# Score units in the third batch, four accumulations on ScalarE and GpSimd, two combining tiles in attention's first period

## The chip, the cores and the metric

The kernel runs on one core of a Trainium2 chip. The metric is the device time of one execution in microseconds (us), lower is better. The engines have names of their own: TensorE (PE in the profile, with PEld for its weight loads) multiplies matrices, VectorE (DVE) and ScalarE (ACT) work on tiles and can read PSUM, where TensorE writes, GpSimd (POOL) works on tiles in SBUF alone, SyncE (SP) issues most of the DMAs.

## The reference

One macaron block on x of shape (4, 512, 128), in float32:

```python
x = x + 0.5 * ffn(layernorm(x), ...)
x = x + attention(layernorm(x), Wq, Wk, Wv, Wo)
x = x + 0.5 * ffn(layernorm(x), ...)      # the same weights
```

`ffn` is a mixture of eight experts (128 to 128 to 128, SiLU) of which each token takes the two with the largest router probabilities, plus a shared expert with a gate and an up projection whose output is scaled by a sigmoid of its own. All experts are computed for all tokens; the weight of an expert that a token doesn't take is zero. `attention` has 16 heads of 8 columns, is causal, and takes a slope times the distance off each score.

## The kernel before, in words

The work is in three blocks: first feed-forward block, attention, second feed-forward block. Each engine has its own program, written out in order by hand; semaphores connect them. Nothing is reordered by a planner: what stands behind a waiting instruction on its engine waits too.

**A feed-forward block** runs over four batches of 512 tokens (j = 0 to 3 in the first block, 4 to 7 in the second). A batch has nine combining tiles n = 0 to 8 (eight experts and the shared one), numbered i = 9 j + n. For each n TensorE makes a hidden tile two steps ahead (`hidden`, lines 802 to 816, three matmuls of 512 columns), ScalarE applies SiLU (`silu`, L416), TensorE multiplies by the second weight (`combine`, L834, eight matmuls, into one of three banks, `Y_BANK[i % 3]`), and VectorE scales each token's row by its coefficient and adds it onto X (`accumulate`, L632, four operations of 128x128). The semaphore `y_used` counts tiles added; a combining tile waits until the tile three before it was added and its bank is free. `gate_up` (L617) makes the gated input of tile 8. GpSimd computes the coefficients (`route`, `coef`).

**The projections** of attention's first two batches, and a part of the layer norms, are done in between. `PROJECT_PE`, `PROJECT_ACT` and `PROJECT_DVE` say in which step (j, n) each engine does its part. For the second batch of attention: TensorE projects at (3, 3) and (3, 5); ScalarE takes the high part of the result (`high_qk`, L449) at (3, 4) and (3, 6); VectorE subtracts it (`rest_qk`, L675) at (3, 3) and (3, 5); ScalarE takes the middle part (`middle_qk`, L453) at (3, 5) and (3, 7); GpSimd the low part (`low_qk`, L348); SP writes the three parts to DRAM (`write_parts`, L217 to L223) and later reads them back in the layout that the score matmuls want (`read_rows`, L235).

**Attention** runs over 16 groups G of four heads (four groups a batch), in 17 periods n. A period has ten slots i. In each slot `score_pair(n, i)` interleaves, on TensorE, one transposed unit of group n (`scores_t_steps`, L932, whose exponentials ScalarE takes, L477) with one score unit of group n + 2 (`score_steps`, L905, of which VectorE takes the masked row maxima, `maxima`, L700). A score unit is 512 columns in one or two matmuls, and u = 10 G + i. The maxima of a group are split in three bf16 parts by GpSimd (`split_smax`), transposed by TensorE (`transpose_smax`, L918; for group 0 at step (3, 7), for group n + 1 in slot (n, 3)), copied by ScalarE (`copy_smax`, L483; for group 0 at (3, 8)) and written by SP into rows of the queries (`maximum_rows`, L244). The transposed units of a group wait for these rows (`nm_rows`). GpSimd masks the exponentials (L367), TensorE weighs the values with them (`weigh_values`, L964) in the next period, into `O_BANK`, which is bank 5.

**What sets the order around the change.** The score units of groups 0 and 1 (u = 0 to 19) are issued early, inside the fourth batch of the first block: after each step n `early_scores(n)` says how many, by

```python
EARLY_STEPS = {0: 2, 1: 2, 2: 2, 3: 2, 4: 2, 5: 2, 6: 2, 7: 2, 8: 4}
```

They alternate between banks 2 and 7, so a unit waits until the masks of the unit two before it are done. On VectorE the order of a step is: gating (at n = 7), accumulation, other work of the step, statistics of a layer norm (at n = 6), masks of the early units. Attention's period 0 begins on TensorE when all 36 tiles of the first block are added (`pe.wait_ge(y_used, C * B)`, L1004), and its first transposed unit waits for the maximum rows of group 0. On SP the order is: write the parts of batches 0 and 1 (the rows of batch 0 are read in between), `maximum_rows(0)`, and then period by period. Slot (0, 2) also holds the value projection of the first batch (`values`, 12 matmuls), slot (0, 9) the transposes of a layer norm's result.

## Time and profile before

| what | value |
|---|---|
| device time, median of 3 runs | 321.56 us (320.27 to 321.93) |
| the profiled execution: its own time | 318.92 us |
| the profiled execution: span of its instructions | 317.2 us |
| TensorE busy | 285.7 us, 90% |
| VectorE busy | 251.5 us, 79% |
| ScalarE busy | 171.6 us, 54% |
| GpSimd busy | 125.5 us, 40% |
| granted TensorE clock, mean | 0.973 of full |

Busy time is the time in which an engine executes at least one instruction. Matmuls are pipelined and their ends are modelled, so a busy TensorE is not TensorE at its peak. The profile of one execution is read by the page, by the instructions of an engine in order of time, by groups of instructions and by windows; every time of an instruction is counted from the start of the span. The chain of work that ended last runs for 59% of the span on TensorE and for 18% on VectorE. The first block lasts to about 100 us, attention to about 247 us, the second block to the end.

### The profile page before, as it was taken

What the parts mean: (1) busy time and instruction counts of PE and PEld (TensorE: products, weight loads), DVE (VectorE), ACT (ScalarE), POOL (GpSimd) and SP (SyncE); (2) the same over time, 40 slices, a digit from 0 to 9 for tenths busy, and PEclk for the clock granted to TensorE, in tenths of its full rate; (3) what the DMA queues carried; (4) which work ended last, traced back from release to release, by engine and by line L of the source; (5) the groups of instructions that cost most, each with busy time, mean ns of one, the idle gap of its engine ahead of it and who ended that gap; (6) DMA issues with size and microseconds to landing.
All of it is one profiled execution on the core that took longest, in us unless ns stands there. A gap on an engine that the chain in (4) does not pass through costs nothing.

```text
span 317.2 us, 7138 instructions
## 1 busy us (share of the span) xinstructions
PE 285.7 (90%) x2328; PEld 185.2 (58%) x2328; DVE 251.5 (79%) x1049; ACT 171.6 (54%) x326; POOL 125.5 (40%) x255
## 2 busy tenths in 40 slices
PE   0898998989986998999799999999999999999994
PEld 0687886977652534334343344333444798889894
DVE  3659798788999678998788989999522697988775
ACT  2423432532442667977688888787888243334330
POOL 1385255406143225546414544565622352520200
PEclk9999999999997569999999999999999999999999
DMA  6910000650050014421104411110000001000011
GB/s 170 238 27 3 0 2 2 208 166 25 4 198 2 2 54 151 151 54 52 53 19 136 152 54 52 53 55 2 2 4 2 1 2 33 2 21 16 1 33 35
DMA packets 20669, 17.73 MB, mean 56 GB/s; under 512 B 2461, under 2 KB 19421, under 8 KB 20573
## 3 DMA queue, kind: packets, MB, share of 16 engines
q1 hardware_dynamic: 19912, 17.05, 18.0%
q8 instruction: 19, 0.31, 0.4%
q10 hardware_dynamic: 720, 0.23, 0.3%
q14 instruction: 18, 0.14, 0.1%
HBM read 9.74 MB, written 7.34 MB: 54 GB/s over the span
## 4 chain that ended last, share of the span: by engine, by line
PE 59%; DVE 18%; POOL 8%; issue 7%; ACT 4%; DMA 2%; SPq 1%; DVEq 0%; POOLq 0%; ACTq 0%
PE bank L834 14%; PE bank L964 10%; PE bank L932 9%; PE bank L772 7%; DVE X L632 6%; PE bank L774 5%; PE bank L773 5%; DVE masked_s L700 4%; POOL probs L367 3%; DVE stats L569 2%; PE bank L905 2%; DMA X<-in_x 2%; PE bank L974 2%; ACT probs L477 2%; PE bank L987 1%
## 5 line engine op out<-in xcount | busy, mean ns | idle before, releaser
L700 DVE CUSTOM_DVE_ANT_0 masked_s<-bank,causal_sb 128x512 f32<-128x512 f32 (+3 forms) x256 | 109.7, 485 | 12.9 <-PE bank L905 12.8
L477 ACT ACTIVATE probs<-bank 128x512 f32<-128x512 f32 x160 | 89.7, 602 | 27.7 <-PE bank L932 26.8
L632 DVE SCALAR_TENSOR_TENSOR X<-bank,coef,X 128x128 f32<-128x128 f32 x288 | 80.7, 342 | 20.9 <-PE bank L834 14.5
L834 PEld LDWEIGHTS bank<-w_sb,act 128*128 128x128 f32 x512 | 67.7, 193 | 5.6
L834 PE MATMUL bank<-w_sb,act 128*128 128x128 f32 x512 | 68.0, 276 | 0.0
L367 POOL TENSOR_SCALAR_AFFINE_SELECT probs<-probs 128x512 f32<-128x512 f32 x64 | 39.7, 635 | 67.9 <-ACT probs L477 67.9
L905 PE MATMUL bank<-KA,QA 54*128 54x512 bf16 (+3 forms) x256 | 59.2, 318 | 6.7 <-DVE smax L700 6.0
L416 ACT ACTIVATE act<-bank 128x512 f32<-128x512 f32 x72 | 41.8, 594 | 40.1 <-PE bank L774 40.1
L932 PE MATMUL bank<-QA,KA 57*128 57x128 bf16 (+3 forms) x256 | 58.9, 315 | 0.2
L964 PE MATMUL bank<-probs,VA 128*32 128x256 f32 (+2 forms) x640 | 52.6, 396 | 1.4 <-issue 0.9
L772 PE MATMUL bank<-XH,w_hi 128*128 128x512 f32 x88 | 42.8, 486 | 5.1 <-DVE gated L617 2.3
L932 PEld LDWEIGHTS bank<-QA,KA 57*128 57x128 bf16 x256 | 17.2, 96 | 40.3 <-ACT probs L477 21.3
L774 PE MATMUL bank<-XH,w_lo 128*128 128x512 f32 x88 | 35.5, 403 | 0.0
L773 PE MATMUL bank<-XL,w_hi 128*128 128x512 f32 x88 | 35.2, 400 | 0.0
L905 PEld LDWEIGHTS bank<-KA,QA 54*128 54x128 bf16 x256 | 16.5, 96 | 20.0 <-DVE smax L700 18.2
L772 PEld LDWEIGHTS bank<-XH,w_hi 128*128 128x128 f32 x88 | 17.1, 195 | 12.1 <-DVE gated L617 4.8
L964 PEld LDWEIGHTS bank<-probs,VA 128*32 128x32 f32 x640 | 13.9, 109 | 16.9 <-issue 13.7
L700 DVE DVE_READ_ACCUMULATOR2_ANT smax<- 128x1 f32 x256 | 21.1, 83 | 0.0
L774 PEld LDWEIGHTS bank<-XH,w_lo 128*128 128x128 f32 x88 | 16.9, 193 | 4.0
L304 POOL TENSOR_TENSOR above<-above 128x128 f32<-128x128 f32 (+2 forms) x24 | 8.1, 336 | 24.9 <-DVE above L607 23.6
L773 PEld LDWEIGHTS bank<-XL,w_hi 128*128 128x128 f32 x88 | 17.2, 196 | 0.2
L409 ACT ACTIVATE XH<-bank 128x512 fp32r<-128x512 f32 x12 | 7.2, 597 | 18.7 <-PE bank L788 18.7
(77 smaller groups left out, 320.1 us busy)
## 6 DMA issues: line engine op xcount, KB each, us to landing
qk_scratch<-qk_parts SPq DMA_DIRECT2D x8, 384.0 KB, 2.6
QA<-qk_scratch SPq DMA_DIRECT2D x32, 96.0 KB, 2.3
KA<-qk_scratch SPq DMA_DIRECT2D x32, 96.0 KB, 2.3
qk_scratch<-qk_parts SPq DMA_DIRECT2D x8, 256.0 KB, 2.9
qk_scratch<-qk_parts SPq DMA_DIRECT2D x8, 128.0 KB, 2.8
QA<-smaxT SPq DMA_DIRECT2D x64, 3.0 KB
out_x<-X SPq DMA_DIRECT2D x4, 256.0 KB, 2.3
X<-in_x SPq DMA_DIRECT2D x3, 256.0 KB, 6.2
```

The costliest lines, as they stand in the source:

```text
L367: nc.gpsimd.affine_select(out=blk, in_=blk, compare_op=ALU.is_ge, fill=0.0, base=0, pattern=[[0, GH], [1, P]], channel_multiplier=-1).then ...
L416: nc.scalar.activation(act[:, i % 3, :], H_BANK[(HID * j + n) % 2][:, :], ACT.Silu).then_inc(act_ready, 1)
L477: nc.scalar.activation(dst, src, ACT.Exp).then_inc(exp_done, 1)
L632: m = nc.vector.scalar_tensor_tensor(X[:, b * NT + t, :], Y_BANK[i % 3][:, t * P:(t + 1) * P], coef[:, j % 2, t, n:n + 1], X[:, b * NT + t ...
L700: r = nc.vector.tensor_tensor_reduce(masked_s[:, u % 4, off:off + n], bank[:, off:off + n], causal_sb[:, S - n:S], 1.0, -3e38, ALU.add, AL ...
L772: nc.tensor.matmul(dst, w_h, m_h, start=True, stop=False)
L773: nc.tensor.matmul(dst, w_h, m_l, start=False, stop=False)
L774: return nc.tensor.matmul(dst, w_l, m_h, start=False, stop=True)
L834: m = nc.tensor.matmul(Y_BANK[i % 3][:, r], a, w2_sb[:, n, :], start=True, stop=True)
L905: m = nc.tensor.matmul(dst[:, off:off + n], QA[b % 2][r, h // 2, qt * P:(qt + 1) * P], KA[b % 2][r, h // 2, 0:n], start=True, stop=True, s ...
L932: m = nc.tensor.matmul(T_BANK[u % 3][:, off:off + WID[kt]], KA[b % 2][r, h // 2, kt * P:(kt + 1) * P], QA[b % 2][r, h // 2, kt * P:S], sta ...
L964: m = nc.tensor.matmul(O_BANK[32 * hh:32 * hh + 32, q0:q1], VA[b % 2][:, kt, GH * g + hh, :], probs[G % 2][:, hh, at + q0:at + q1], start= ...
```

## The change

It has three parts, and waits that go with them.

1. The early score units are laid out over steps (j, n) instead of steps of the fourth batch alone: one unit after step 7 and two after step 8 of the third batch, and 2, 2, 1, 2, 2, 2, 2, 2, 2 after the nine steps of the fourth. There are 20 as before.
2. The tiles n = 1, 3, 5 and 6 of the fourth batch (`SIDE`) are not accumulated by VectorE. ScalarE scales each into a tile of SBUF (`scale_side`, four activations of 128x128 with a scale per token), one step later, behind the SiLU of that step. GpSimd adds the four to each other (`add_side`, 128x512, three times) and in period 0 adds their sum onto X (`finish_ffn3`, once more 128x512). `y_count(i)` is the number of tiles before i that VectorE adds; all waits on `y_used` go by it.
3. The tiles n = 7 and 8 of the fourth batch (`DEFERRED`) are multiplied by TensorE in period 0, after slots (0, 1) and (0, 4), into bank 5, and VectorE accumulates them one slot later, behind its masks. Period 0 no longer waits for them. The first weighing of values waits until they are added, since it writes bank 5 too; the statistics of the fourth batch's layer norm wait for `finish_ffn3`.

The diff, cut to its core:

```diff
+        gated, side = sb("gated", [P, S]), sb("side", [P, 3, NT, D])
...
-        EARLY_STEPS = {0: 2, 1: 2, 2: 2, 3: 2, 4: 2, 5: 2, 6: 2, 7: 2, 8: 4}
+        EARLY_STEPS = {(2, 7): 1, (2, 8): 2, (3, 0): 2, (3, 1): 2, (3, 2): 1, (3, 3): 2, (3, 4): 2, (3, 5): 2,
+                       (3, 6): 2, (3, 7): 2, (3, 8): 2}
+        SIDE = tuple(C * (B - 1) + n for n in (1, 3, 5, 6))
+        DEFERRED = {(0, 1): C * B - 2, (0, 4): C * B - 1}
+        def y_bank(i):
+            return banks[5] if i in DEFERRED.values() else Y_BANK[i % 3]
+        def y_count(i):
+            return i - sum(s < i for s in SIDE)
...   (GpSimd)
+            def add_side(k):
+                pool.wait_ge(side_scaled, k + 1)
+                if k >= 2:
+                    pool.wait_ge(side_added, k - 1)
+                nc.gpsimd.tensor_tensor(side[:, 0], side[:, 0], side[:, 1 + (k - 1) % 2], ALU.add).then_inc(side_added, 1)
+            def finish_ffn3():
+                pool.wait_ge(side_added, len(SIDE) - 1)
+                pool.wait_ge(y_used, y_count(C * B))
+                xt = X[:, (B - 1) * NT:B * NT, :]
+                nc.gpsimd.tensor_tensor(xt, xt, side[:, 0], ALU.add).then_inc(x_ffn3, 1)
...
                     if kind == 0 and b == B - 1:
                         low_qk(1, 0)
+                        add_side(1)
                         split_smax(0)
                         low_qk(1, 1)
+                        add_side(2)
...
                         layer_norm(ln_index(*after), after[1])
                     if kind == 0 and b == B - 1:
+                        add_side(3)
                         split_smax(1)
...
                     split_smax(n + 2)
+                if n == 0:
+                    finish_ffn3()
...   (ScalarE)
                             silu(C * j + n)
+                        if C * j + n - 1 in SIDE:
+                            scale_side(SIDE.index(C * j + n - 1))
...
+            def scale_side(k):
+                i = SIDE[k]
+                j, n = divmod(i, C)
+                ac.wait_ge(y_ready, i + 1)
+                if k == 0:
+                    ac.wait_ge(coef_ready, j + 1)
+                if k >= 3:
+                    ac.wait_ge(side_added, k - 2)
+                dst = side[:, 0 if k == 0 else 1 + (k - 1) % 2]
+                for t in range(NT):
+                    m = nc.scalar.activation(dst[:, t, :], y_bank(i)[:, t * P:(t + 1) * P], ACT.Copy,
+                                             scale=coef[:, j % 2, t, n:n + 1])
+                m.then_inc(side_scaled, 1)
...   (VectorE)
-                        accumulate(C * j + n)
+                        if C * j + n not in SIDE and C * j + n not in DEFERRED.values():
+                            accumulate(C * j + n)
...
                         maxima(n + 2, i)
+                    if (n, i - 1) in DEFERRED:
+                        accumulate(DEFERRED[n, i - 1])
...   (TensorE)
-                if i >= 3:
-                    pe.wait_ge(y_used, i - 2)
+                if i in DEFERRED.values():
+                    pe.wait_ge(y_used, y_count(i))
+                elif i >= 3:
+                    if i - 3 in SIDE:
+                        pe.wait_ge(side_scaled, SIDE.index(i - 3) + 1)
+                    else:
+                        pe.wait_ge(y_used, y_count(i - 2))
...
-                        combine(j, n)
+                        if C * j + n not in DEFERRED.values():
+                            combine(j, n)
...
-                        if j == B - 1:
-                            for G, k in early_scores(n):
-                                score_pair(G - 2, k)
+                        for G, k in early_scores(j, n):
+                            score_pair(G - 2, k)
...
+                    if G == 0:
+                        pe.wait_ge(y_used, y_count(C * B))
...
                     if n == 0 and i == 0:
-                        pe.wait_ge(y_used, C * B)
+                        pe.wait_ge(y_used, y_count(C * B - 2))
+                        pe.wait_ge(side_scaled, len(SIDE))
                     score_pair(n, i)
+                    if (n, i) in DEFERRED:
+                        combine(*divmod(DEFERRED[n, i], C))
```

## Rows read from the trace of the kernel before

**Rows 1.** The page, the span in 40 slices: granted TensorE clock in tenths

```profile
PEclk9999999999997569999999999999999999999999
```

**Rows 2.** Windows: start:end length, busy PE, PEld, DVE, ACT, POOL, clock, DMA, GB/s

```profile
72.70:83.10 10.40, 10.02 (x66) 7.46 (x64) 9.22 (x35) 2.54 (x5) 5.16 (x11) 1.00 0.00 0
83.10:91.60 8.50, 7.84 (x46) 5.51 (x44) 8.36 (x35) 4.15 (x8) 2.89 (x6) 1.00 0.29 95
91.60:100.50 8.90, 5.86 (x36) 3.55 (x36) 8.86 (x43) 2.07 (x3) 3.66 (x5) 0.92 0.24 90
100.50:111.20 10.70, 10.46 (x54) 5.41 (x52) 7.58 (x39) 6.65 (x12) 3.27 (x8) 0.50 0.00 1
111.20:121.80 10.60, 10.60 (x92) 4.47 (x91) 8.33 (x37) 7.54 (x14) 3.54 (x9) 0.77 0.27 77
121.80:130.70 8.90, 7.87 (x87) 3.10 (x86) 7.12 (x30) 7.28 (x15) 3.97 (x10) 1.00 0.37 116
```

**Rows 3.** VectorE in order of time (start, length), and the masks' group of the page

```profile
75.00 1.13 DVE L632 SCALAR_TENSOR_TENSOR X<-bank,coef,X 128x128 f32<-128x128 f32 x4 [0.89 <-POOL coef L313]
...
77.25 1.12 DVE L632 SCALAR_TENSOR_TENSOR X<-bank,coef,X 128x128 f32<-128x128 f32 x4
78.29 0.68 DVE L700 CUSTOM_DVE_ANT_0 masked_s<-bank,causal_sb 128x512 f32<-128x512 f32 x1
...
89.33 0.69 DVE L675 SCALAR_TENSOR_TENSOR qk_rest<-bank,qk_parts 128x512 f32<-128x512 f32 x1
...
101.56 0.69 DVE L700 CUSTOM_DVE_ANT_0 masked_s<-bank,causal_sb 128x512 f32<-128x512 f32 x1
...
L700 DVE CUSTOM_DVE_ANT_0 masked_s<-bank,causal_sb 128x512 f32<-128x512 f32 (+3 forms) x256 | 109.7, 485 | 12.9 <-PE bank L905 12.8
```

**Rows 4.** TensorE in order of time, third batch

```profile
63.64 1.05 PE L834 MATMUL bank<-w_sb,act 128*128 128x128 f32 x8
64.45 0.48 PE L772 MATMUL bank<-XH,w_hi 128*128 128x512 f32 x1
...
71.08 0.50 PE L772 MATMUL bank<-XH,w_hi 128*128 128x512 f32 x1 [0.94 <-DVE gated L617]
```

**Rows 5.** ScalarE's groups by shape: busy us, mean ns of one

```profile
L477 ACT ACTIVATE probs<-bank 128x512 f32<-128x512 f32 x160 | 89.7, 602 | 27.7 <-PE bank L932 26.8
...
L424 ACT ACTIVATE sl<-shifted 128x32 f32<-128x32 f32 x8 | 1.7, 215 | 0.0
...
L405 ACT ACTIVATE w_hi<-w_raw 128x256 fp32r<-128x256 f32 x1 | 0.4, 400 | 0.0
```

**Rows 6.** Middle part, low part, write of the parts, maximum rows, in order of time

```profile
90.05 0.63 ACT L453 ACTIVATE qk_parts<-qk_rest 128x512 bf16<-128x512 f32 x1 [0.27 <-DVE qk_rest L675]
...
90.76 1.15 POOL L348 TENSOR_TENSOR qk_parts<-qk_rest,qk_parts 128x512 bf16<-128x512 f32 x1 [1.43 <-ACT qk_parts L453]
...
91.94 0.34 SPq L221 DMA_DIRECT2D qk_scratch<-qk_parts  x1
...
92.80 0.47 SPq L223 DMA_DIRECT2D qk_scratch<-qk_parts  x1
94.43 2.84 SPq L244 DMA_DIRECT2D QA<-smaxT  x4
```

**Rows 7.** DMA from 94.4 to 99.4 us, GB/s in 40 slices of 0.125 us

```profile
GB/s 303 320 352 238 17 0 0 0 0 0 0 16 8 0 0 0 0 25 0 0 0 0 25 0 0 0 0 0 25 0 0 0 0 0 0 0 0 0 0 0
```

**Rows 8.** Period 0 in order of time: TensorE, SP, a piece of the chain

```profile
100.53 0.63 PE L932 MATMUL bank<-QA,KA 57*128 57x512 bf16 x1
...
102.57 0.47 PE L772 MATMUL bank<-w_hi,XH 128*128 128x128 f32 x1
...
105.32 0.60 PE L932 MATMUL bank<-QA,KA 57*128 57x512 bf16 x1
...
106.17 0.59 PE L918 MATMUL bank<-id_b,smax 128*12 128x128 bf16 x4 [0.24 <-ACT VA L460]
...
107.29 0.42 PE bank L932 x2
...
107.40 2.69 SPq L244 DMA_DIRECT2D QA<-smaxT  x4
```

More of the change, by code:

```diff
@@ L65, in macaron_block @@
         act = sb("act", [P, 3, S])
-        gated = sb("gated", [P, S])
+        gated, side = sb("gated", [P, S]), sb("side", [P, 3, NT, D])
         qk_rest = sb("qk_rest", [P, 2, S])
@@ L104, in macaron_block @@
         y_ready, y_used = sem("y_ready"), sem("y_used")
+        side_scaled, side_added, x_ffn3 = sem("side_scaled"), sem("side_added"), sem("x_ffn3")
         qk_ready, qk_high, qk_sub = sem("qk_ready"), sem("qk_high"), sem("qk_sub")
@@ L139, in macaron_block, with early_scores @@
         EARLY = 2 * NU
-        EARLY_STEPS = {0: 2, 1: 2, 2: 2, 3: 2, 4: 2, 5: 2, 6: 2, 7: 2, 8: 4}
+        EARLY_STEPS = {(2, 7): 1, (2, 8): 2, (3, 0): 2, (3, 1): 2, (3, 2): 1, (3, 3): 2, (3, 4): 2, (3, 5): 2,
[6 more added lines that the diff above has]
+            return i - sum(s < i for s in SIDE)
         def score_bank(u):
             return banks[(2, 7)[u % 2]] if u < EARLY else banks[(2, 7, 0)[(u - EARLY) % 3]]
-        def early_scores(n):
-            first = sum(EARLY_STEPS[k] for k in EARLY_STEPS if k < n)
-            return [divmod(u, NU) for u in range(first, first + EARLY_STEPS.get(n, 0))]
+        def early_scores(j, n):
+            first = sum(EARLY_STEPS[k] for k in EARLY_STEPS if k < (j, n))
+            return [divmod(u, NU) for u in range(first, first + EARLY_STEPS.get((j, n), 0))]
         def score_units(g):
@@ L263, in _ @@
             for b in range(B):
-                sp.wait_ge(y_used, C * (B + b + 1))
+                sp.wait_ge(y_used, y_count(C * (B + b + 1)))
                 sp.dma_start(out[b].rearrange("(t p) d -> p t d", p=P), X[:, b * NT:(b + 1) * NT, :]).then_inc(stored, 16)
@@ L309, in route @@
                 if j >= 2:
-                    pool.wait_ge(y_used, C * (j - 1))
+                    pool.wait_ge(y_used, y_count(C * (j - 1)))
+                if j - 2 == B - 1:
+                    pool.wait_ge(side_scaled, len(SIDE))
                 nc.gpsimd.tensor_scalar(coef[:, j % 2, :, E], th[:, :], 1.0, 0.25, ALU.add, ALU.mult)
@@ L564, in moments @@
                 elif kind == 1:
-                    v.wait_ge(y_used, C * (b + 1))
+                    v.wait_ge(y_used, y_count(C * (b + 1)))
+                    if b == B - 1:
+                        v.wait_ge(x_ffn3, 1)
                 else:
@@ L629, in accumulate @@
                 if i >= 1:
-                    v.wait_ge(y_used, i)
+                    v.wait_ge(y_used, y_count(i))
                 for t in range(NT):
-                    m = nc.vector.scalar_tensor_tensor(X[:, b * NT + t, :], Y_BANK[i % 3][:, t * P:(t + 1) * P],
+                    m = nc.vector.scalar_tensor_tensor(X[:, b * NT + t, :], y_bank(i)[:, t * P:(t + 1) * P],
                                                        coef[:, j % 2, t, n:n + 1], X[:, b * NT + t, :], ALU.mult, ALU.add)
@@ L666, in ffn @@
                             moments(*after)
-                        if j == B - 1:
-                            for G, i in early_scores(n):
-                                maxima(G, i)
+                        for G, i in early_scores(j, n):
+                            maxima(G, i)
             def rest_qk(b, i):
@@ L833, in combine @@
                     a = gated[:, r] if n == E else act[:, i % 3, r]
-                    m = nc.tensor.matmul(Y_BANK[i % 3][:, r], a, w2_sb[:, n, :], start=True, stop=True)
+                    m = nc.tensor.matmul(y_bank(i)[:, r], a, w2_sb[:, n, :], start=True, stop=True)
                 m.then_inc(y_ready, 1)
@@ L860, in ffn @@
                             part(*of)
-                        if j == B - 1:
-                            for G, k in early_scores(n):
-                                score_pair(G - 2, k)
+                        for G, k in early_scores(j, n):
+                            score_pair(G - 2, k)
                         if j == B:
```

## Prediction, written before the changed kernel was run

> **What bounds the kernel now.** I read the slices of the page first. TensorE's clock is full in all of them but three in a row [rows 1], which is where the first block ends and attention begins; so I read that stretch in windows, stage by stage [rows 2]. In the first half of the fourth batch TensorE is the full engine (10.02 us of 10.40). In 91.6 to 100.5 it is VectorE (8.86 of 8.90), TensorE works 5.86 us, and the clock falls at the end of that stretch (mean 0.92). Attention's period 0 then runs wholly at the lower level, 1.2 GHz (clock 0.50), with TensorE busy 10.46 of 10.70; period 1 gets the 2.4 GHz back about half way (0.77); period 2 needs 8.90 us at full clock. So two things cost time here: VectorE's load before attention, and the slow clock that its starving of TensorE leaves behind. From period 2 on nothing in the diff touches the order except one small GpSimd addition long before its use, so a shift at 121.8 us is a shift of the end.
>
> **The change part by part.** Prices: a tile's accumulation holds VectorE 1.04 us (77.25 to the next mask at 78.29), a score unit's masks 0.69 us (109.7 us over 160 units) [rows 3]. On TensorE a combining tile takes 0.81 us at full clock (63.64 to 64.45) [rows 4].
>
> Units 0 to 2 in the third batch. Unit 0 is issued where TensorE waits 0.94 us for the gated tile anyway [rows 4]: free. Units 1 and 2 stand before the next hidden tile; unit 2 needs the bank of unit 0, so TensorE loses about 0.7 us there, and saves a part of it where the pair stood before, one step later. VectorE's masks fill the 0.89 us that it waits for the coefficients (the accumulation at 75.00) [rows 3] and run over by 0.3 us. All together between 0 and +0.7 us at this place; I take +0.3, which the next part absorbs. The rows that unit 0 reads were issued long before; their last issue of group 0 precedes unit 0 by some 3.7 us.
>
> First half of the fourth batch. TensorE is the bound there, so what VectorE sheds buys nothing. I walked through it tile by tile: each unit waits for the masks two units back, each of the two subtractions of the projection (L675) for TensorE's projection and a ScalarE copy; the second of them, at 89.33 before [rows 3], comes at 89.2. Gain 0.1 us.
>
> Second half. From that subtraction VectorE had 12.2 us to the end of the last early mask (101.56, where the next unit begins) [rows 3]. Of these, three accumulations (3.1 us) and two of the ten units (1.3) are gone; subtraction, statistics and gating stay. 7.8 us, done at 97.0. TensorE issues its last early unit when the mask two before it is done, and is free at 95.9; the first matmul of attention stood at 100.53 [rows 8]. If nothing else held it, this would be -4.6 us, the far end.
>
> What holds it next: the maximum rows of group 0. SP issues them behind the three writes of the second batch's key parts, these wait for GpSimd's low part, that for ScalarE's middle part, and this now stands behind the copy of the fourth side tile, which waits for the combining tile (3,6). By my walk that tile ends at 90.2. Side copy 1.0, and 0.1 until it begins: 91.3. Middle part 0.63: 91.9. Low part 1.15: 93.05. Three issues on SP, 1.33: 94.4 [rows 6]. The rows were issued from 94.43 before, and their four transfers show in the DMA bins up to 98.0, 3.6 us after the first issue [rows 7]. So they land at 98.0 again, hidden before by VectorE, now the last thing that period 0 waits for: start at 98.1, -2.4 us. The GpSimd sums of the side tiles (as large as the low part, so some 1.15 us each) stand behind the low part, or in front of the first split of maxima, which is done some 4 us before TensorE transposes it. I take 0; if the second sum slipped in front of the low part it would be +1.15.
>
> The side copies. No activation of 128x128 is in the trace. Below lies the 128x32 (215 ns), above the 128x256 (400 ns) [rows 5]; I take 0.25 us, nearer the smaller, since neighbours overlap: 1.0 us for a tile of four. Ends: 0.86, with four of the smaller, and 2.4 us, at the 602 ns of 512 columns. Two such tiles stand in the rows' chain (before the second high part, and before the middle part), so the ends move the start of period 0 by -0.3 and +2.8 us.
> The Trainium skill, ScalarE: Activation LUTs, section "What ACT_TABLE_LOAD costs", says that an activation costs 186 ns plus 0.833 ns a column and each per-partition pointer operand some 93 ns more. The first agrees with the 215 ns of the 128x32 row; the side copies carry their scale as such a pointer, which no activation here does. By that page a tile would be 1.2 us (an estimate), the start of period 0 98.5 and the whole 0.4 us less gain.
>
> The waits that come with them. A side copy waits for a combining tile that TensorE issues a hidden tile after the one whose SiLU ScalarE would take next; so that SiLU moves back by the tile and the copy, some 1.8 us. Who needs it is TensorE, a combining tile, a pair and a hidden tile later (0.81, 0.4 and about 0.8 us, and the masks' waits between them): 0, and at most 4 x 0.5 us if the copies reach their upper end. TensorE's waits on the side copies before it takes a bank again, and GpSimd's on the copies, find them done a step earlier. The first weighing of values, in period 1, waits for the second deferred accumulation, which VectorE does half a period before: 0. GpSimd's last addition, 1.15 us, falls in the idle time between its masks of periods 0 and 1.
>
> The two deferred tiles. They put 16 matmuls into period 0: 1.6 us at full clock, 3.3 us at the lower one (half pace), and two accumulations on VectorE, which waited for TensorE in this period and hides them. Bounds 0 and 3.3.
>
> The clock. TensorE is nearly idle from 92.6 to 98.1 in the new order (four units and four transposes in 5.5 us), sparser than the stretch before which the clock fell last time, so it falls again, before period 0 begins. The question is how long it stays. Before, it stayed low through all of period 0 and into period 1. There the tile (0,1) now joins the pairs and the value projection, and the tile (0,4) makes the stretch after the transposes of maxima longer by 1.65 us of dense matmuls (106.7 to 110.1 before). I take it to come back inside period 0.
>
> The sum, by period 0's own rows [rows 8]: start 98.1; two pairs at 0.43 (the chain's 0.42 for a pair's two transposed score matmuls; the first ones waited for masks before, no longer), tile 1.65, pair 0.43, value projection 2.75 (102.57 to 105.32), pair, ScalarE's copy and the transposes (105.32 to 106.17 before): transposes at 104.55. Rows of group 1 issued 1.23 us behind (107.40 against 106.17), landed 3.6 us later: 109.4. Period 1 begins at 109.6 with the clock back at about 107, at 110.7 with it back at the end of period 0, instead of 111.2. Period 1 at full clock: 8.9 as period 2, and 0.6 for its value projection, 9.5 instead of 10.6. Together -2.7 and -1.6; middle -2.2 us. The profiled execution took 318.92 us (span 317.2 and 1.7 around it), 2.6 below the median of the runs, 321.56; I put the shift on the median: 319.4 us. Half a per cent, 1.6 us, is about what a measurement tells from no change.
>
> **The rivals.** (a) The clock stays low as long as before, into period 1. For it: the value projection kept TensorE busy without a break from 102.57 to 105.9 and the clock did not rise. Then transposes at 104.55 leave 1.65 + 6 x 0.43 + 1.1 us of the XN transposes and 0.5 of their own: period 1 at 111.2 as before, later parts alike: 0.0, 321.6 us. Against it: more dense work than before.
> (b) The clock doesn't fall: the rows come as soon as TensorE is free. Period 0 then takes 8.6 us from 98.1 (pairs 0.25, tile 0.81, projection 1.4, ScalarE's copy 0.75, rows' chain 4.85), period 1 9.5: 116.2 for 121.8, -5.6 us, 316.0. Against it: the idle stretch above.
> (c) Slower: ScalarE's side copies sit in front of the second high part and the middle part, and cost the upper end, 2.4 us a tile. The rows land 2.4 to 2.8 us later, the start gains nothing, and the two tiles are paid at the low clock: with 2.4, period 1 at 113.6 and +2.4 us, 324.0. It decides from a start of period 0 later than 99.7. For it: ScalarE takes them in order, and three engines and a queue follow. Against it: the row of 128x256.
> (d) The early units don't get their rows in time in the third batch: the four reads of group 0 come in a stretch where the DMA is busy. TensorE would wait there up to 1 us, where it is the bound: 320.4.
>
> **How the numbers follow.** Forecast 0.55 (its own range 318.1 to 320.6), (a) 0.20, (b) 0.08, (c) 0.12, (d) 0.05. Faster by over 0.5%: four fifths of the forecast, all of (b), some of (d): 0.54. Slower: (c) and a little of (a): 0.14. The rest, 0.32: within. The range takes in (b) with part of the 2.6 us between profile and median, and half of (c): 315.2 to 323.0.
>
> **What would show it.** Right: VectorE's last early mask near 97.0; attention's first matmul near 98.1, released by the maximum rows; the clock low at that moment and full again before period 1 begins near 110; period 1 of 9.5 us; masks and the last statistics unmoved in relation to the periods. Wrong: a start of period 0 before 97 (the rows' chain is shorter than I think) or after 99.7; a clock that never falls, or that is low in half of period 1; side copies of over 0.35 us; the projection's second subtraction later than 90; TensorE waiting for rows in the third batch.

## The result, and the profile of the changed kernel

The changed kernel takes 324.3 us (median of 20 runs, 319.69 to 328.5), the kernel before 321.8 us beside it on the same chip (20 runs, 319.6 to 325.31). Executions of one kernel fall into a faster and a slower kind, and every ratio in this document is that of the faster ones alone, while the medians are those of all. The ratio is 1.0068 (95% interval [1.004, 1.0096]): slower by 0.7%, where 319.4 us and a gain had been forecast. The profiled execution took 322.08 us with a span of 320.3 (before 318.92 and 317.2), so the two traces differ by 3.1 us; the medians differ by 2.5 and the runs, by the ratio, by 2.2. The traces show the sign of the difference and about its size.

The page of the changed kernel, granted TensorE clock in 40 slices of the span, against [rows 1]:

```profile
PEclk9998999999995579999999999999999999999999
```

The low stretch lies in the same three slices (13 to 15) and is deeper in the first of them: the clock falls earlier. (The 8 in the fourth slice lies ahead of everything that the diff touches; the kernel without part 3, below, has a full clock there, and its gated tile of the third batch starts at 72.16 us, here at 72.17.) The windows by stage, cut where the stages of [rows 2] end in the new trace (start:end length, busy PE, PEld, DVE, ACT, POOL, clock, DMA share, GB/s):

```profile
72.90:83.40 10.50, 10.50 (x67) 7.82 (x68) 8.97 (x37) 4.01 (x12) 5.24 (x11) 1.00 0.00 0
83.40:92.00 8.60, 7.74 (x47) 5.48 (x46) 5.91 (x21) 5.14 (x14) 3.24 (x6) 1.00 0.29 94
92.00:99.90 7.90, 3.87 (x19) 1.31 (x18) 6.27 (x35) 3.78 (x8) 6.36 (x7) 0.69 0.27 101
99.90:114.30 14.40, 13.14 (x68) 8.57 (x68) 7.98 (x35) 6.66 (x12) 3.26 (x8) 0.58 0.10 28
114.30:124.90 10.60, 10.52 (x92) 4.37 (x91) 8.93 (x41) 7.46 (x15) 5.27 (x10) 0.84 0.14 41
124.90:133.80 8.90, 7.87 (x87) 3.10 (x86) 7.12 (x30) 7.28 (x15) 3.97 (x10) 1.00 0.35 116
```

The first two stages are about as long as before (10.5 and 8.6 us, 10.4 and 8.5 before). VectorE did get lighter: in the second it is busy for 5.91 us where it was 8.36, in the third for 6.27 where it was 8.86. Yet attention begins at 99.90 instead of 100.53, only 0.63 us earlier, with TensorE busy for 3.87 us of 7.90. Period 0 is 14.4 us long instead of 10.7, period 1 is 10.6 as before, and from period 2 on nothing differs. So -0.63 + 3.74 + 0.0 = +3.1 us: all of the span's difference is there at the start of period 2, and what makes it is period 0.

TensorE in order of time in the changed kernel (start, length, in brackets the idle time before it and what ended that), against [rows 8]:

```profile
99.90 0.58 PE L992 MATMUL bank<-QA,KA 57*128 57x512 bf16 x1 [2.39 <-DMA QA<-smaxT]
...
100.96 2.07 PE L894 MATMUL bank<-w_sb,act 128*128 128x128 f32 x8
102.97 0.60 PE L992 MATMUL bank<-QA,KA 57*128 57x512 bf16 x1
...
108.16 2.07 PE L894 MATMUL bank<-w_sb,gated 128*128 128x128 f32 x8
...
113.40 0.28 PE L965 MATMUL bank<-KA,QA 54*128 54x256 bf16 x1 [1.02 <-DVE smax L753]
...
114.31 0.39 PE L992 MATMUL bank<-QA,KA 57*128 57x512 bf16 x1
...
124.92 0.39 PE L992 MATMUL bank<-QA,KA 57*128 57x512 bf16 x1
```

The lines at 99.90, 114.31 and 124.92 begin periods 0, 1 and 2. Three things are to be seen. Before period 0 TensorE waits 2.39 us with nothing to do, for the maximum rows. The two deferred tiles then hold it for 2.0 us each (100.96 to 102.97, 108.16 to 110.17). And at the end of period 0 it waits another 1.02 us for masks.

The clock over those moments (windows of 2 us, columns as above):

```profile
94.00:96.00 2.00, 0.90 (x4) 0.22 (x4) 2.00 (x10) 1.96 (x3) 1.92 (x4) 0.77 0.35 138
96.00:98.00 2.00, 1.21 (x4) 0.25 (x4) 1.99 (x13) 0.11 (x1) 1.92 (x2) 0.50 0.69 258
...
110.00:112.00 2.00, 2.00 (x18) 0.94 (x17) 1.16 (x6) 1.20 (x3) 0.00 (x0) 0.50 0.02 5
112.00:114.00 2.00, 0.98 (x10) 0.44 (x8) 2.00 (x12) 1.15 (x3) 1.22 (x2) 0.97 0.66 185
114.00:116.00 2.00, 1.92 (x14) 0.49 (x14) 2.00 (x12) 1.91 (x5) 1.08 (x3) 0.89 0.04 12
116.00:118.00 2.00, 2.00 (x19) 0.75 (x22) 2.00 (x8) 0.85 (x2) 1.67 (x4) 0.50 0.00 0
```

The granted clock is at its lower level (0.50, 1.2 GHz) when both deferred tiles run, returns near 112, inside period 0, and falls a second time near 116, after the 112-to-114 window in which TensorE was busy for only 0.98 us.

The wait for the maximum rows is in the chain that ended last (start, length, what), against [rows 6, 7]:

```profile
93.30 1.16 POOL qk_parts L381
...
94.48 0.34 SPq L235
...
95.86 0.78 SPq L258
...
98.06 1.71 DMA QA<-smaxT
...
99.90 0.58 PE bank L992
```

That is the chain the prediction named (low part, three writes, rows), in which every step up to the issue of the rows is 1.3 to 1.5 us later than it was walked: rows issued at 95.86 and not at 94.4. ScalarE shows where that begins:

```profile
88.75 1.14 ACT L492 ACTIVATE side<-bank,coef 128x128 f32<-128x128 f32 x4 [2.49 <-PE bank L894]
89.76 0.61 ACT L500 ACTIVATE qk_parts<-bank 128x512 bf16<-128x512 f32 x1
...
91.56 1.14 ACT L492 ACTIVATE side<-bank,coef 128x128 f32<-128x128 f32 x4 [0.70 <-PE bank L894]
92.57 0.65 ACT L504 ACTIVATE qk_parts<-qk_rest 128x512 bf16<-128x512 f32 x1
```

A side copy, itself waiting for a combining tile, stands in front of the second high part, so that VectorE's second subtraction starts at 90.41 (89.33 before, 89.2 forecast). The next one stands in front of the middle part, and ScalarE waits 0.70 us for its combining tile, (3, 6), before it can begin at 91.56 (90.3 forecast). What made that tile late is told below, where the prediction is gone through.

### The profile page after: what moved, and what is told of

Same layout as the page of the kernel before. It is cut to its first block, busy times and chain, and to the rows that moved or that the text cites. A ratio compares the mean times of both kernels' runs of the same rounds, so it can differ in the third digit from the quotient of the medians.

```text
span 320.3 us, 7144 instructions
## 1 busy us (share of the span) xinstructions
PE 288.2 (90%) x2328; PEld 187.3 (58%) x2328; DVE 247.4 (77%) x1033; ACT 175.5 (55%) x342; POOL 130.4 (41%) x259
## 4 chain that ended last, share of the span: by engine, by line
PE 60%; DVE 14%; POOL 9%; issue 7%; ACT 4%; DMA 2%; SPq 2%; DVEq 0%; POOLq 0%; ACTq 0%
PE bank L894 16%; PE bank L1026 10%; PE bank L992 8%; PE bank L827 7%; PE bank L829 5%; PE bank L828 5%; DVE X L685 5%; DVE masked_s L753 3%; POOL probs L400 2%; DVE stats L622 2%; DMA X<-in_x 2%; PE bank L965 2%; PE bank L1036 2%; ACT probs L528 2%; POOL qk_parts L381 1%
## 5 line engine op out<-in xcount | busy, mean ns | idle before, releaser
L685 DVE SCALAR_TENSOR_TENSOR X<-bank,coef,X 128x128 f32<-128x128 f32 x272 | 76.2, 342 | 20.0 <-PE bank L894 14.4
L894 PEld LDWEIGHTS bank<-w_sb,act 128*128 128x128 f32 x512 | 69.2, 197 | 6.5 <-issue 0.8
L894 PE MATMUL bank<-w_sb,act 128*128 128x128 f32 x512 | 69.5, 280 | 0.0
L992 PE MATMUL bank<-QA,KA 57*128 57x128 bf16 (+3 forms) x256 | 57.9, 311 | 2.6 <-DMA QA<-smaxT 2.4
L827 PEld LDWEIGHTS bank<-XH,w_hi 128*128 128x128 f32 x88 | 17.2, 196 | 10.5 <-issue 4.2
```

Source lines behind the costliest of these rows:

```text
L685: m = nc.vector.scalar_tensor_tensor(X[:, b * NT + t, :], y_bank(i)[:, t * P:(t + 1) * P], coef[:, j % 2, t, n:n + 1], X[:, b * NT + t, :] ...
L827: nc.tensor.matmul(dst, w_h, m_h, start=True, stop=False)
L894: m = nc.tensor.matmul(y_bank(i)[:, r], a, w2_sb[:, n, :], start=True, stop=True)
L992: m = nc.tensor.matmul(T_BANK[u % 3][:, off:off + WID[kt]], KA[b % 2][r, h // 2, kt * P:(kt + 1) * P], QA[b % 2][r, h // 2, kt * P:S], sta ...
```

## The experiments

The theory after the result: parts 1 and 2 (units in the third batch, side copies) help a little and are then held by the maximum rows; part 3 (the two deferred tiles) takes work out of a stretch where TensorE waits and puts it into a period in which it is full, at the lower clock. The main rival: the side copies in the rows' chain are what costs.

Each kernel is compared with the kernel before, run beside it on the same chip, whose median was 321.55 to 321.77 there. Two kernels are compared by their ratios to it; 0.1% is 0.3 us.

### The changed kernel without part 3

```
-        DEFERRED = {(0, 1): C * B - 2, (0, 4): C * B - 1}
+        DEFERRED = {}
-                        pe.wait_ge(y_used, y_count(C * B - 2))
+                        pe.wait_ge(y_used, y_count(C * B))
```

> The changed kernel with its third part undone: tiles 7 and 8 of the fourth batch are multiplied and added in their steps, period 0 waits for them; the early units and the side tiles stay. Theory A (TensorE waits for the maximum rows in front of period 0 anyway, so the two tiles were free where they stood and are paid in full in period 0): first transposed matmul at 100.2 to 101 (99.9 in the changed kernel), period 0 shorter by 3.5 to 4.1 us than its 14.4, no 2.07 us groups of the combining line in it; about -3 us against the changed kernel at a like clock, -0.5 to +0.5 against the one before. Rival (the time follows the low clock alone): period 0 stays near 14 us, the time stays within 1 us of the changed kernel's.

Measured: 320.28 us, ratio 0.9962 [0.9924, 1.0001], so 1.1% or some 3.4 us less than the changed kernel. Its TensorE at the beginning of periods 0, 1 and 2, and its windows before period 0 and in it:

```profile
99.91 0.58 PE L992 MATMUL bank<-QA,KA 57*128 57x512 bf16 x1 [1.57 <-DMA QA<-smaxT]
...
110.04 0.60 PE L992 MATMUL bank<-QA,KA 57*128 57x512 bf16 x1
...
119.94 0.39 PE L992 MATMUL bank<-QA,KA 57*128 57x512 bf16 x1
```
```profile
92.00:99.90 7.90, 5.04 (x35) 3.27 (x34) 7.87 (x42) 3.79 (x8) 6.35 (x7) 0.96 0.27 101
99.90:110.00 10.10, 9.85 (x52) 5.58 (x52) 6.83 (x35) 6.50 (x12) 3.78 (x9) 0.50 0.00 1
```

Period 0 starts at the same moment, released by the same rows: the two tiles fit into the wait in front of it, which goes from 2.39 to 1.57 us. It then takes 10.13 us instead of 14.41, though its clock is low from end to end, and period 1 (to 119.94) 9.9 instead of 10.61. So part 3 costs 4.98 us at the start of period 2, and what it takes away in front of period 0 is worth nothing. It even empties TensorE there (3.87 us busy of 7.90, 5.04 without part 3), and the clock falls at 95.1 instead of 99.2. The rival falls: the side copies are all in here. (Of the 4.98 us the ends of the two traces show 2.0, because this one has low stretches late in attention that the other has not; see what stays open.)

### Part 3 alone, on the kernel before

Against the changed kernel, cut to its core (the waits and sums of the side tiles go too):

```
-        EARLY_STEPS = {(2, 7): 1, (2, 8): 2, (3, 0): 2, (3, 1): 2, (3, 2): 1, (3, 3): 2, (3, 4): 2, (3, 5): 2,
-                       (3, 6): 2, (3, 7): 2, (3, 8): 2}
-
-        SIDE = tuple(C * (B - 1) + n for n in (1, 3, 5, 6))
+        EARLY_STEPS = {(3, 0): 2, (3, 1): 2, (3, 2): 2, (3, 3): 2, (3, 4): 2, (3, 5): 2, (3, 6): 2, (3, 7): 2, (3, 8): 4}
+
+        SIDE = ()
```

> The kernel before with the third part alone: tiles 7 and 8 of the fourth batch go into period 0, VectorE adds them there; early units and the other accumulations as before. Theory A: VectorE's stretch in front of attention loses two accumulations (2.1 us), the rows land near 98.0, first transposed matmul at 98.5 instead of 100.53; period 0 then carries two groups of 2.07 us at the lower clock level and waits once for masks behind an accumulation: 13.5 to 14.4 us instead of 10.67; in all +1 to +2 us against the kernel before at a like clock. Rival (the third part costs only beside the side tiles): within 0.5 us of the kernel before or faster.

Measured: 322.58 us, 1.0052 [1.0022, 1.0082]: slower by itself, within the expected loss. Its profiled execution was an unusually long one (327.6 us), so its periods are not compared with the others (period 0 takes 15.63 us in it, at the lower clock throughout, where 13.5 to 14.4 had been expected). Its beginning is read: the rows are issued at 95.42, a write of the parts ahead of them having taken 1.37 us on SP, and period 0 starts at 99.78, behind the last early units, where 98.5 had been expected. The start was missed; the sign and the size of the loss were not.

### Part 1 alone, and part 2 alone

The first has the new table of early units on the kernel before; the second is the changed kernel with the old table and nothing deferred.

> The kernel before with the first part alone: three score units move into the third batch, the rest is laid out as in the changed kernel. VectorE's stretch between the second subtraction and the end of the early masks loses two units (1.3 us), no accumulation. Theory A: last early mask near 100.2 instead of 101.56, first transposed matmul at 99.2 to 99.6 instead of 100.53, -1.0 to -1.3 us at a like clock. Rival (the third batch pays for what it takes): hidden tiles of the fourth batch start 0.5 us later and stay so, first transposed matmul within 0.4 us of 100.53.

> The kernel before with the second part alone: four accumulations go to ScalarE and GpSimd; units and the last two tiles as before. VectorE loses one accumulation between the second subtraction and the end of the early masks, and three ahead of it, where TensorE is the bound. Theory A: VectorE ends 1.0 us earlier, but the rows, behind two side copies of 1.14 us, are issued at 95.9 and land at 99.5: first transposed matmul at 99.9 to 100.2, -0.4 to -1.2 us at a like clock. Rival (VectorE is the bound up to attention, so that all four count): first transposed matmul at 97 or earlier, -3 us or more.

Measured: 320.77 us each, ratios 0.9955 [0.9917, 0.9994] and 0.9968 [0.9932, 1.0005]. The first transposed matmul of each, part 1 alone and then part 2 alone:

```profile
99.94 0.58 PE L931 MATMUL bank<-QA,KA 57*128 57x512 bf16 x1 [0.48 <-DVE X L633]
```
```profile
99.95 0.37 PE L991 MATMUL bank<-QA,KA 57*128 57x512 bf16 x1
```

Part 1 alone starts 0.3 us later than the 99.2 to 99.6 it was given, part 2 alone within its bounds. Alone, together (99.91) or with part 3 as well (99.90), period 0 starts at 99.9. But the last wait is another one each time: VectorE's last accumulation in the one, the early units just ahead of it in the other, the maximum rows where both are in. By the ratios the gains are 0.5%, 0.3% and, together, 0.4%, each with an interval of some 0.4% to either side: whether they add can't be told from the times. In the traces they do, by the start of period 2, at 121.81 before, 121.16 and 120.69 with one part and 119.94 with both, though the start of period 0 is the same.

### The rows ahead of the second key write on SP's queue

```
             for b in range(2):
                 write_parts(b, 0)
+                if b == 1:
+                    maximum_rows(0)
                 write_parts(b, 1)
 ...
-            maximum_rows(0)
```

> The changed kernel with one edit on SP: the maximum rows of group 0 are issued ahead of the write of the second batch's key parts instead of behind it. Theory A (the rows stand in SP's queue behind the parts, which stand behind the side copy): rows issued at 94.6, when ScalarE's copy ends, instead of 95.86; first transposed matmul at 98.6 instead of 99.9, the end 1.3 us earlier. Rival (the rows' queue is not what period 0 waits for): first matmul unmoved at 99.9.

Measured: rows issued at 94.63 (95.86 in the changed kernel), and TensorE

```profile
98.67 0.58 PE L993 MATMUL bank<-QA,KA 57*128 57x512 bf16 x1 [1.16 <-DMA QA<-smaxT]
```

The start follows the issue by 4.04 us in both (95.86 to 99.90, 94.63 to 98.67): the rows are what period 0 waits for. The median is 323.43 us, 1.0035 [0.9995, 1.0074]; 0.3%, about 1 us, less than the changed kernel, for 1.2 us at the start. The interval does not separate it from the changed kernel.

### ScalarE's projection parts ahead of the side copy in each step

```
-                        if C * j + n - 1 in SIDE:
-                            scale_side(SIDE.index(C * j + n - 1))
 ...
                             part(*of)
+                        if C * j + n - 1 in SIDE:
+                            scale_side(SIDE.index(C * j + n - 1))
```

> The changed kernel with one edit on ScalarE: in each step the projection's part (high, middle) stands in front of the side copy instead of behind it. Theory A: high part of the second projection's second half at 89.2 instead of 89.76, its middle part at 90.5 instead of 92.57, low part at 91.8, parts written from 91.8, rows issued at 94.6 (then bound by ScalarE's copy of them), first transposed matmul at 98.6, the end 1.3 us earlier, as with the queue's edit. Rival (the side copies cost ScalarE's time as such, wherever they stand): SiLU and the copy of the maxima move back by as much, first matmul at 99.9 or later.

Measured: rows issued at 94.24, and TensorE

```profile
98.27 0.58 PE L992 MATMUL bank<-QA,KA 57*128 57x512 bf16 x1 [1.71 <-DMA QA<-smaxT]
```

The place of the side copies in ScalarE's order is worth 1.6 us of the start, about the 1.8 us by which the forecast start (98.1) was too early: it takes the wait for the combining tile (3, 6) out of the rows' chain. The median is 323.13 us, 1.0007 [0.9969, 1.0046], 0.6% or 2 us under the changed kernel: still no gain over the kernel before. Even with the forecast start, part 3 loses it again: period 0 takes 14.42 us and period 1 11.74, with the clock falling anew at 113.4, so that period 2 starts only 0.5 us earlier than in the changed kernel (124.43).

### Unread matmuls that keep TensorE busy before period 0

Matmuls of 512 columns into a free bank that nobody reads are put in front of the last early units and of period 0, in the changed kernel (21 of them) and in the kernel before (10).

```
+            def filler(k):
+                for _ in range(k):
+                    nc.tensor.matmul(banks[4][:, :], w_hi[:, 0:F], w_hi[:, 0:S], start=True, stop=True)
 ...
+                                filler({16: 1, 17: 2, 18: 4, 19: 2}[NU * G + k])
                             score_pair(G - 2, k)
 ...
+                        filler(12)
                     score_pair(n, i)
```

(In the kernel before the bank is `MISC`, the numbers are 2, 1, 6 and 1, and none stands in front of period 0.)

> The changed kernel with 21 matmuls of 512 columns added on TensorE, whose result nobody reads: 9 in the waits in front of the last four early units, 12 (some 2.6 us at full clock) in the wait for the maximum rows. They cost nothing while they fit in the waits. Theory B (the low clock of period 0 follows from the idle stretch in front of it): the clock stays full, first transposed matmul at 99.9 to 100.3, the two tiles 1.0 us each instead of 2.07, period 0 at 9 to 10 us instead of 14.4, period 1 at 9.5 instead of 10.6: -5 to -6 us. Rival (the clock falls for another reason, as at a fixed place): clock falls near 95 as before, and the time is the same or up to 1 us more.

> The kernel before with 10 matmuls of 512 columns whose result nobody reads, in the waits ahead of the last four early units (2, 1, 6, 1). Nothing else is changed. Theory B: the clock doesn't fall at 99, first transposed matmul at 100.5 to 100.8 as before, period 0 at 8.6 to 9.2 instead of 10.67, period 1 at 9.0 to 9.5 instead of 10.61: -2.5 to -3.5 us against the kernel before. Rival (the clock falls whatever stands there, or the periods are not TensorE's): low clock in periods 0 and 1 as before, or a full clock and the same periods: within 0.5 us of the kernel before, or slower by up to 0.5.

Measured: on the changed kernel 321.57 us, 0.9974 [0.9935, 1.0013], 0.9% or 3 us less than without the unread matmuls, where 5 to 6 had been expected; on the kernel before 319.47 us, 0.9933 [0.99, 0.9967], a gain of 2.2 us, a little short of the expected 2.5 to 3.5. The changed kernel with them, TensorE:

```profile
98.01 3.03 PE L953 MATMUL bank<-w_hi 128*128 128x512 f32 x12
100.97 0.39 PE L999 MATMUL bank<-QA,KA 57*128 57x512 bf16 x1
...
101.51 1.16 PE L894 MATMUL bank<-w_sb,act 128*128 128x128 f32 x8
102.60 0.39 PE L999 MATMUL bank<-QA,KA 57*128 57x512 bf16 x1
...
110.00 0.28 PE L972 MATMUL bank<-KA,QA 54*128 54x256 bf16 x1 [1.17 <-DVE smax L753]
...
111.22 0.60 PE L999 MATMUL bank<-QA,KA 57*128 57x512 bf16 x1
```

and its clock:

```profile
104.00:108.00 4.00, 3.36 (x35) 2.16 (x33) 2.83 (x13) 2.74 (x6) 0.65 (x1) 1.00 0.00 1
108.00:112.00 4.00, 2.77 (x16) 1.35 (x17) 4.00 (x23) 2.75 (x7) 1.86 (x3) 0.81 0.37 102
```

With the clock kept, a deferred tile takes 1.09 us (101.51 to 102.60) and period 0 10.25 us, not 14.41. The start is 1.1 us late because twelve were too many. Most of the rest of what was missed is the same wait for masks as in the changed kernel, here 1.17 us. VectorE in front of it:

```profile
108.14 1.12 DVE L685 SCALAR_TENSOR_TENSOR X<-bank,coef,X 128x128 f32<-128x128 f32 x4
109.18 0.28 DVE L753 CUSTOM_DVE_ANT_0 masked_s<-bank,causal_sb 128x128 f32<-128x128 f32 x1
```

The second deferred accumulation pushes back the masks for which TensorE waits (without part 3 TensorE does not wait there), and behind that wait the clock falls after all. In the kernel before, the same trick gives a period 0 at full clock; periods 0 and 1 there:

```profile
101.00:109.80 8.80, 6.73 (x55) 3.45 (x53) 7.63 (x37) 6.88 (x13) 3.36 (x8) 1.00 0.01 2
109.80:119.80 10.00, 10.00 (x93) 4.42 (x93) 8.09 (x35) 6.96 (x13) 3.44 (x8) 0.83 0.30 82
```

Period 0 starts 0.5 us later than before and shrinks from 10.7 to 8.8 us, 0.86 of it a wait at its end for the next group's maximum rows. Period 1 takes 10.0 us, where 9 to 9.5 had been expected: the clock falls in it.

### Parts 1 and 2 with the rows pulled forward, without and with unread matmuls

```
         DEFERRED = {}
         (maximum_rows(0) on SP as in the queue experiment)
-                          (3, 7): (transpose_smax, 0)}
+                          (3, 6): (transpose_smax, 0)}
 (ScalarE: the projection's parts ahead of the side copies as in the order experiment, and
  copy_smax(0) in step (3, 7), behind the middle part and ahead of the side copy)
 second kernel: + filler, 1 ahead of the gated tile, 3 and 1 ahead of the last two units, 2 ahead of period 0
```

> Parts one and two without the deferral (as in the run with the third part undone), and the maximum rows of group 0 made earlier: transposed after step (3, 6), copied behind the middle part in step (3, 7), the projection's parts ahead of the side copies on ScalarE, the rows ahead of the second batch's key parts on SP. Theory A: rows issued at 92.5 instead of 95.88, landed at 96.5; then period 0 waits for the last accumulation instead (98.85 in that run): first transposed matmul at 99.0 instead of 99.91, the end about 1 us earlier than that run's, -2 to -2.5 us against the kernel before at a like clock. Rival (the clock takes it back, as in the runs with the queue's and the order's edit): earlier start, same time within 0.5 us.

> The same with 7 matmuls of 512 columns whose result nobody reads, in TensorE's waits of the last step of the fourth batch: 1 ahead of the gated tile, 3 and 1 ahead of the last two early units, 2 in front of period 0. Theory B (the idle stretch lowers the clock): it stays full into period 0, first transposed matmul at 99.0 to 99.4, period 0 at 8.6 to 9.2 instead of 10.1, period 1 at 9.0 instead of 9.9: 1.5 to 2.5 us faster than the same without them. Rival (seven are too few): clock falls before 100 and the time is that of the run without them.

Measured: without, 319.57 us, 0.992 [0.9882, 0.9957]; rows issued at 92.25, period 0 from 98.41 (expected 99.0) to 109.02, at the lower level for most of it. With, 317.24 us, 0.9869 [0.9812, 0.9926], the lowest of all: 1.3%, some 4.2 us, under the kernel before (its interval overlaps those of the same kernel without and of the kernel before with unread matmuls). The second kernel's stages (91.0 to period 0, period 0, period 1):

```profile
91.00:98.80 7.80, 7.18 (x43) 4.39 (x42) 7.76 (x40) 3.98 (x10) 6.89 (x7) 1.00 0.28 105
98.80:107.30 8.50, 7.12 (x54) 3.76 (x53) 7.33 (x36) 6.48 (x13) 3.42 (x9) 0.88 0.01 3
107.30:117.90 10.60, 10.60 (x93) 4.47 (x95) 8.12 (x35) 7.32 (x14) 4.70 (x9) 0.77 0.27 77
```

Now VectorE is full again up to period 0 (7.76 of 7.80) and the rows no longer hold period 0. Seven unread matmuls of some 0.25 us keep the clock until late in period 0, which takes 8.44 us. Period 1 is as slow as before: the low stretch (105.3 to 112.1) was shortened and moved there rather than removed.

## Why the prediction was wrong, step by step

The place was right: all of the difference is there at the start of period 2, TensorE bound the first half of the fourth batch, and VectorE's load before attention was what the change took away: from its second subtraction (90.41) to the end of the last early mask (98.3) it needs 7.9 us, 7.8 forecast. Also right: the maximum rows became the last wait, the clock fell before period 0, and it came back inside period 0.

**"Start at 98.1, -2.4 us": 99.90, -0.63.** The chain was the right one; the time at which it begins was not. The walk had the combining tile (3, 6) end at 90.2, half a microsecond earlier than before. It ended at 91.5, and with it the side copy, the middle part, the low part, the writes and the rows came 1.3 to 1.5 us late. The tile in the kernel before, in the changed one, with part 1 alone and with part 2 alone:

```profile
89.72 1.05 PE L834 MATMUL bank<-w_sb,act 128*128 128x128 f32 x8
```
```profile
90.47 1.06 PE L894 MATMUL bank<-w_sb,act 128*128 128x128 f32 x8
```
```profile
90.69 1.05 PE L834 MATMUL bank<-w_sb,act 128*128 128x128 f32 x8
```
```profile
89.98 1.05 PE L893 MATMUL bank<-w_sb,act 128*128 128x128 f32 x8
```

So the step that failed is "+0.3, which the next part absorbs" together with "Gain 0.1 us". With the new table two more early units stand ahead of this tile on TensorE (14, not 12), and TensorE is the full engine there. The delay is not absorbed: the tile starts 0.75 us later than before, 0.97 with part 1 alone and 0.26 with part 2 alone, where the walk had a gain of half a microsecond.

The second subtraction came at 90.41, past the "later than 90" that the prediction itself set as the sign of an error: TensorE's projection ahead of it is 0.75 us later as well (88.47, 87.72 before), and the side copy in front of the high part adds 0.3. The chain doesn't wait for it, since the middle part waits for the side copy.

The price of a side copy in this chain was right: the instruction behind one starts 1.01 us after it (91.56 to 92.57), 1.0 forecast. One activation takes 368 ns, which is over the 0.35 us set as a sign of an error, and four take 1.14 us, but the last of them overlaps with the next instruction:

```profile
L492 ACT ACTIVATE side<-bank,coef 128x128 f32<-128x128 f32 x16 | 4.6, 368 | 6.8 <-PE bank L894 6.8
```

The Trainium skill (ScalarE: Activation LUTs, "What ACT_TABLE_LOAD costs") made a tile 1.2 us, an estimate, and the measured 1.14 lies nearer to it than to my 1.0. The rest of the 1.8 us, 0.4, is behind the issue. DMA from 95.8 to 100.8 us, GB/s in 40 slices of 0.125 us, against [rows 7]:

```profile
GB/s 418 418 418 385 361 344 426 360 426 320 295 369 271 33 0 0 0 25 0 0 0 0 8 16 0 0 0 0 25 0 0 0 0 0 0 0 0 0 0 0
```

The last of the four small transfers shows in the slice that ends at 99.4, 3.6 us after the issue, as forecast; the chain has the DMA last until 99.77 (98.06 and 1.71), and the first matmul starts 0.5 us after that slice and not 0.1.

**"The two deferred tiles: 1.6 us at full clock, 3.3 at the lower": the decisive term, 4.0 us and more.** Three things were wrong in it. The size: 0.81 us a tile came from one pair of rows ([rows 4]); at full clock the tile holds TensorE for 1.09 us (101.51 to 102.60 with the unread matmuls), and 2.0 at the lower level, as the changed kernel's two tiles show. The place: the sum counted what the tiles add to period 0 and never asked what their removal in front of it gains. It gains nothing: TensorE waits there, 2.39 us without them and 1.57 us with them, and the start was 99.9 both ways. And the cover: VectorE "hides" the two accumulations. It hides the first. The second runs from 111.53 to 112.6, ahead of the masks that the last pieces of period 0 need, and costs TensorE 1.02 us at 113.40. By the kernel without part 3 the whole part costs 4.28 us in period 0 (14.41 against 10.13) and 0.7 us in period 1.

**"Period 1 of 9.5 us": 10.6.** The clock came back at about 112, 2.3 us before period 1, as forecast, but not for the reason given, "more dense work". The low stretch is as long as before, some 17 us (95.1 to 112.1; 99.1 to 116.1 before), and ended earlier because it began earlier; without the two dense tiles it lasted 13.7 us (99.2 to 112.8). This part of the forecast was right by luck. What was not foreseen is the second fall near 116. It comes after TensorE stood for 1.02 us; in the kernel with 21 unread matmuls a fall follows the like wait of 1.17 us. Without part 3 there is no such wait, no second fall before period 2, and period 1 takes 9.9 us, so parts 1 and 2 do bring part of that gain. That the wait alone caused the second fall was not tried.

Together: start +1.8, period 0 +2.4 (14.41 against the 12.0 between 98.1 and the middle of 109.6 and 110.7), period 1 +1.1: 5.3 us, from -2.2 to +3.1.

**The rivals.** (c) had the sign, its threshold (a start later than 99.7) and its end, 324.0. It had half of the mechanism: the side copies do sit in front of the high and middle parts, but hold them up for 1.0 us a tile and not 2.4, and with the same start the kernel without part 3 is no slower than before. The price was the deferred tiles, which (c) counted only as an addition. (a), no change, did not occur: the low stretch was as long as before, as (a) has it, but the clock came back before period 1, and the time rose. (b) was shut out by the idle 2.39 us, but the kernels with unread matmuls show what a kept clock is worth. (d) did not occur.

What stays open: single runs of one kernel spread by 5 us and more (319.6 to 325.31 before). In the profiled executions the longer ones have a lower mean clock (0.973 for the 318.92 us of before, 0.963 for the 322.08 us of after, 0.989 for the 315.04 us of the best kernel), and several have further low stretches late in attention, as the page of part 2 alone shows:

```profile
PEclk9999999999997589999999999797999999999999
```

From the start of period 2 to the end a trace without any of them takes 195.4 us (before, after, the last two kernels), the one with one 197.0 (order) and those with two 198.3 to 198.4 (without part 3, the queue, parts 1 and 2 alone, both first kernels with unread matmuls); part 3 alone, with three, takes 199.8. That is some 1.5 us each. So the spans of two traces can hide or feign such a difference, and the starts of period 2 compare the kernels better. What decides whether a late low stretch comes was not found.

## What to carry to other kernels

Before work is moved off an engine, look at whether that engine waits where the work stands: there it costs nothing, and in a period in which the same engine is full it costs its whole length, at the clock of that period. When a load is lifted from one engine, walk the next chain through every queue in its new order, from the engine that is full: what is put ahead of a tile there is not absorbed, and the instructions that lift the load may wait for that tile. And keep TensorE supplied ahead of a dense stretch: here unread matmuls alone brought 0.7%, while the two tiles moved out of the sparse stretch left it emptier and brought its clock down 4 us earlier.

## What the runs showed of the hardware

A combining tile of eight 128x128 fp32 matmuls holds TensorE for 1.09 us at the upper level and 2.0 us at the lower, 1.8 times as long. Once the clock had fallen, it stayed at 0.50 through stretches in which TensorE's records are nearly without a gap: 10.46 us busy of 10.70 in period 0 of the kernel before [rows 2], 2.00 of 2.00 us at 110 to 112 in the changed kernel. In both traces the low stretch lasted some 17 us, in others 6.8 (the kernel with seven unread matmuls) and 13.7 (without part 3). GpSimd's sum of two 128x512 fp32 side tiles takes 1.26 to 1.29 us, and the low part of the same shape 1.15, the row by which it had been priced.
